# The token tile of step s+2 turned at a step's head through the projection bank, and copied before the SiLU

## What is computed

```python
x = L0_attn_x                                   # 8 x 512 x 256, float32
xn = _layernorm(x, axis=-1)
x = x + mamba(xn) + experts(xn)

# mamba: in-projection to 512 (a half is the gate), causal convolution of 4 taps,
# SiLU, projections to B, C (16 each) and dt; then for 16 states of each channel
#   h = h * exp(dt * A) + dt * B * x;   y = sum(h * C) + x * D
# over 512 tokens; y * silu(gate); out-projection; layernorm(out + xn)

# experts: 8 experts, 2 per token, hidden width 1024
logits = silu(xt @ rw1 + rb1) @ rw2 + rb2       # top 2 are kept, softmax over them
h = silu(xt @ we1[e] + be1[e]);  eo = h @ we2[e] + be2[e]
y = xt + sum over the token's 2 experts of weight * eo
```

## Time and profile before

| | us |
|---|---|
| median of 3 timed runs | 930.38 (929.67 to 933.92) |
| the profiled execution's time | 937.38 |
| its span, first to last instruction | 935.0 |
| TensorE busy | 790.0 (84%) |
| VectorE busy | 781.6 (84%) |
| ScalarE busy | 664.7 (71%) |
| GpSimd busy | 601.8 (64%) |

### The profile page before, as it was taken

One profiled execution on the slowest core, in us unless ns is written; L12 is line 12 of the kernel. 1 busy time (PEld: TensorE's weight loads), 2 busy tenths in 40 slices (PEclk: granted clock), 3 DMA queues, 4 the chain that ended last, 5 costly groups with the idle time before them and its releaser, 6 DMA issues.

```text
span 935.0 us, 14382 instructions
## 1 busy us (share of the span) xinstructions
PE 790.0 (84%) x4533; PEld 639.3 (68%) x4533; DVE 781.6 (84%) x774; ACT 664.7 (71%) x1134; POOL 601.8 (64%) x384
## 2 busy tenths in 40 slices
PE   3994859898998899889988998989988998899852
PEld 2662648777776778677866887677767786778741
DVE  6818857997989988997899699969898789969993
ACT  1433677858688778876887779686887788769930
POOL 3571525676478747774777756785687487758861
PEclk9996979998999999989999999999999999999985
DMA  9939446577657876787579775776588667877741
GB/s 298 388 142 343 178 135 222 184 222 226 185 181 220 254 224 204 218 249 217 187 209 260 240 221 176 234 260 197 168 222 281 189 216 205 252 214 235 230 90 22
DMA packets 81927, 201.00 MB, mean 215 GB/s; under 512 B 7936, under 2 KB 41216, under 8 KB 81728
## 3 DMA queue, kind: packets, MB, share of 16 engines
q1 hardware_dynamic: 61424, 171.46, 53.9%
q0 software_dynamic: 19168, 26.59, 15.0%
q10 hardware_dynamic: 1264, 2.05, 0.7%
HBM read 174.38 MB, written 26.61 MB: 215 GB/s over the span
## 4 chain that ended last, share of the span: by engine, by line
PE 32%; DVE 31%; issue 9%; ACT 9%; DMA 8%; SPq 2%; POOL 1%; DVEq 0%; ACTq 0%; POOLq 0%
PE ps_up L1248 14%; DVE ps_drive L954 11%; PE ps_yx L1262 8%; DVE ring L961 8%; DVE ps_drive L947 6%; DMA bc_scratch<-sp 6%; PE ps_fr L1179 4%; ACT L805 3%; DVE xx L928 2%; ACT da L778 2%; PE ps_up L1242 2%; DMA out<-yo,sid 2%; PE ps_fr L1204 1%; SPq L527 1%; DMA xg<-xn_scratch,gid 1%
## 5 line engine op out<-in xcount | busy, mean ns | idle before, releaser
L598 POOL TENSOR_TENSOR y<-y,ring 128x1024 f32<-128x1024 f32 x126 | 326.2, 2589 | 61.6 <-ACT y L769 54.2
L954 DVE TENSOR_TENSOR_SCAN ps_drive<-da,ps_drive 128x1024 f32<-128x1024 f32 x128 | 293.7, 2295 | 57.8 <-ACT da L778 54.2
L1248 PEld LDWEIGHTS ps_up<-xgt,w1s 128*128 128x128 f32 x2272 | 290.9, 200 | 18.8 <-issue 9.6
L1248 PE MATMUL ps_up<-xgt,w1s 128*128 128x128 f32 x2272 | 290.3, 283 | 0.0
L1262 PE MATMUL ps_yx<-w,ht 128*128 x1136 | 270.6, 381 | 0.0
L1262 PEld LDWEIGHTS ps_yx<-w,ht 128*128 128x128 f32 x1136 | 206.4, 191 | 28.7 <-issue 5.0
L587 POOL DMA_INDIRECT out<-yo,sid x71 | 115.6, 1628 | 145.1 <-ACT yo L820 98.2
L805 ACT ACT_TABLE_LOAD x143 | 183.5, 1283 | 2.5
L778 ACT ACTIVATE da<-gd,col 128x511 f32<-128x511 f32 x256 | 168.3, 710 | 0.0
L947 DVE TENSOR_TENSOR ps_drive<-ps_u,rep 128x1024 f32<-128x1024 f32 x128 | 157.4, 1229 | 9.5 <-DVE ring L961 0.5
L961 DVE TENSOR_TENSOR ring<-ps_drive,rep 128x1024 f32<-128x1024 f32 x128 | 156.5, 1223 | 3.9
(11 more groups left out here) (172 smaller groups left out, 720.4 us busy)
## 6 DMA issues: line engine op xcount, KB each, us to landing
w1s<-in_we SPq DMA_DIRECT2D x71, 1024.0 KB, 7.3
rep<-bc_scratch SPq DMA_DIRECT2D x128, 512.0 KB, 4.7
w<-in_we SPq DMA_DIRECT2D x8, 1024.0 KB, 12.0
w<-in_x SPq DMA_DIRECT2D x8, 512.0 KB, 11.1
xn_scratch<-da SPq DMA_DIRECT2D x8, 512.0 KB, 7.0
out<-w POOLq DMA_DIRECT2D x8, 512.0 KB, 6.4
xnt_scratch<-xx SPq DMA_DIRECT2D x8, 512.0 KB, 5.9
xx<-xnt_scratch SPq DMA_DIRECT2D x8, 512.0 KB, 3.5
```

The lines of the kernel that those rows point to most:

```text
L598: pool.tensor_tensor(y[:, :, :], y[:, :, :], ring[:, g % RING, :, :], ALU.add).then_inc(s_sum, 1)
L954: dve.tensor_tensor_scan(states, da[:, g % DECAYS, :, :].rearrange("p k l -> p (k l)"), states, 0.0, ALU.mult, ALU.add).then_inc(s_scanned, 1)
L1248: mm = pe.matmul(bank[:, c * P:(c + 1) * P], w1s[:, q, k, at:at + P], xgt[:, k, :], start=False, stop=(c == 3 and k == KD - 1))
```

## The change

- For tiles whose step of turning is 2 to 8 of a block (`at_head`), `turn_x(s+2)` moves from the middle of `down(s)` to the head of step s, ahead of `up(s+1, 0)`, and writes to the left half of `ps_fr` instead of up0. It waits until all uses of `ps_fr` before it are read and until the copy of tile s+1 is done. Every later use of `ps_fr` waits for the copy of the last tile turned there (`bank_free`).
- For the same tiles `copy_x(s+2)` moves on ScalarE from behind the Exp table to between the SiLU table and `hidden(s+1, 0)`.
- `xgt` gets two buffers, so the copy waits for `up(s)` instead of `up(s+1)`; `xg` gets three, and the gather is issued one tile sooner (s+4 in step s).
- In steps 0 and 1 turning and copying stay where they were.

```diff
+        def at_head(j):
+            return j >= 2 and (j - 2) % STEPS >= 2
...
                 def copy_x(j):
                     act.wait_ge(s_x_turned, j + 1)
-                    if positive(j):
-                        act.wait_ge(s_up_ready, j * 2)
+                    if j >= 2:
+                        act.wait_ge(s_up_ready, j * 2 - 2)
...
                         table_of(ACT.Silu)
+                        if s + 2 < MT and at_head(s + 2):
+                            copy_x(s + 2)
                         for h in range(2):
...
-                    if s + 2 < MT:
+                    if s + 2 < MT and not at_head(s + 2):
                         copy_x(s + 2)
...
+                def bank_free(f):
                     if positive(f):
                         pe.wait_ge(s_fr_read, f)
+                    if last_turned[0] > 0:
+                        pe.wait_ge(s_x_copied, last_turned[0])
+                    used[0] = f + 1
+
+                def project(at, rows_out, f, src):
+                    bank_free(f)
...
                 def turn_x(j):
...
+                    if at_head(j):
+                        pe.wait_ge(s_fr_read, used[0])
+                        pe.wait_ge(s_x_copied, j)
+                        last_turned[0] = j + 1
+                    elif j > 0:
                         pe.wait_ge(s_hidden, j * 2 - 1)
...
+                    if s + 2 < MT and at_head(s + 2):
+                        turn_x(s + 2)
                     if s + 1 < MT:
                         up(b, i + 1, e_next, 0)
```

More of the change, by code:

```diff
@@ L34 @@
 HBUF = 2
+XGS = 3
 assert STEPS % WBUF == 0
@@ L106, in build @@
         xtok = sb("xtok", [P, TB, D])
-        xg = sb("xg", [P, 2, D])
-        xgt = sb("xgt", [P, KD, P])
+        xg = sb("xg", [P, XGS, D])
+        xgt = sb("xgt", [P, 2, KD, P])
         rep = sb("rep", [P, REPS, 2, L])
@@ L471, in build @@
         s_ln_scaled = sem("s_ln_scaled")
-        s_gathered = [sem(f"s_gathered{q}") for q in range(2)]
+        s_gathered = [sem(f"s_gathered{q}") for q in range(XGS)]
         s_x_turned = sem("s_x_turned")
@@ L498, in build, with turned @@
         front = {use: n for n, use in enumerate(uses)}
+        def at_head(j):
+            return j >= 2 and (j - 2) % STEPS >= 2
+        def turned(j):
+            return psum["fr"][:, 0:D] if at_head(j) else tr_x
         def positive(n):
@@ L575, in gather @@
                     pool.wait_ge(s_tables, 2)
[L576 to L579, removed]
+                    if j >= XGS:
+                        pool.wait_ge(s_x_turned, j - XGS + 1)
+                    pool.indirect_dma_start(xg[:, j % XGS, :], None, xn_d[:, :],
+                                            bass.IndirectOffsetOnAxis(ap=gid[:, j:j + 1], axis=0)).then_inc(s_gathered[j % XGS], 16)
                 def scatter(s, b, i):
@@ L638, in step @@
                     s = b * STEPS + i
-                    if s + 3 < MT:
-                        gather(s + 3)
+                    if s + 4 < MT:
+                        gather(s + 4)
                     if i < IN and not (last and i == IN - 1):
@@ L672, in _ @@
                 pool.wait_ge(s_tables, 2)
-                for j in range(3):
+                for j in range(4):
                     gather(j)
@@ L682, in _ @@
                                    accum_op=ALU.add).then_inc(s_out_rows, 16)
-                for q in range(2):
-                    pool.wait_ge(s_gathered[q], 16 * ((MT + 1 - q) // 2))
+                for q in range(XGS):
+                    pool.wait_ge(s_gathered[q], 16 * ((MT + XGS - 1 - q) // XGS))
                 pool.wait_ge(s_scattered, 16 * MT)
@@ L782, in copy_x @@
                     act.wait_ge(s_x_turned, j + 1)
-                    if positive(j):
-                        act.wait_ge(s_up_ready, j * 2)
-                    act.activation(xgt[:, :, :], tr_x.rearrange("p (k c) -> p k c", k=KD), ACT.Copy).then_inc(s_x_copied, 1)
+                    if j >= 2:
+                        act.wait_ge(s_up_ready, j * 2 - 2)
+                    act.activation(xgt[:, j % 2, :, :], turned(j).rearrange("p (k c) -> p k c", k=KD), ACT.Copy).then_inc(s_x_copied, 1)
                 def weights_in(n):
@@ L1196, in proj_out @@
                     pe.wait_ge(s_y_gated, b + 1)
-                    pe.wait_ge(s_fr_read, front["out", b, half])
+                    bank_free(front["out", b, half])
                     for c in range(2):
@@ L1210, in last_out @@
                     if j == 0:
-                        pe.wait_ge(s_fr_read, front["out", B - 2, 1] + 3)
+                        bank_free(front["out", B - 2, 1] + 3)
                     if j in (1, 2):
@@ L1247, in up @@
                         for k in range(KD):
-                            mm = pe.matmul(bank[:, c * P:(c + 1) * P], w1s[:, q, k, at:at + P], xgt[:, k, :],
+                            mm = pe.matmul(bank[:, c * P:(c + 1) * P], w1s[:, q, k, at:at + P], xgt[:, j % 2, k, :],
                                            start=False, stop=(c == 3 and k == KD - 1))
```

8 lines of the change are left out of this document (4 added, 4 removed).

## The result

The changed kernel takes **982.0 us** (median; 979.4 to 989.7, 6 runs) where the kernel before, timed beside it, takes 930.57 us (929.67 to 933.92, 6 runs): a ratio of 1.0545, 95% interval 1.0514 to 1.0575. The change costs some 51 us. Predicted were 969 us with a range of 944 to 992.

What follows compares the result with a forecast made beforehand. It took a PE-ACT-DVE chain through step 2's tap, the store and the tail as the bound. Six blocks at +6.7 us (5.1 loop, 1.6 clock) and block 0 at -1.5 made +38.7 on 930.38: 969 us, range 944 to 992.

Steps and rivals of the forecast that it cites:

- The loop of copies: Steps 2 to 6: ACT's copy and PE's projection take turns; copy to copy 12.3, 13.9, 11.5 and 14.8 us.
- The scatter in step 4: ACT's way from step 4 to 5: a 1.3 us wait for the scatter kept, 11.5 us in all.
- The clock: Behind step 5's new pause of some 6 us, PE's clock falls: 1.6 us a block, from 0 to 3.
- Step 3's pause: PE's pause of 2.7 us in step 3: 0 for the clock, 1.6 us at the upper end.
- Block 0: Copies 4.9 us sooner, store still sets `dt_in(1)`: 2.1 late, tail 2.0 and clock 1.6 less, -1.5 us.
- Block 4: Forecast like all of blocks 1 to 6: 6.7 us longer, near 105.8 us from scan to scan.
- My upper end: 8.3 us plus two us for `gated` and the output projection behind later scatters: 10.3 x 6 = 62 us.
- The tail's gain: Second `dt_in` to next scan: turn waits only for dt's read, copy leaves the chain; 2.0 us a block.
- The way of 12.0 us: Step 7's way to the SiLU in the tail: 12.0 us at full speed, 13.6 before at the lower clock.
- rival D: ACT copies before PE reaches the projection; tail gives 2.0 and clock 1.6 in 7 blocks: 905 us, 9%.
- The block sum: Whole kernel: 6 x 6.7 us for blocks 1 to 6, -1.5 for block 0, 0 for block 7: +38.7.
- The first chain: Step 2's projection waits for ACT's copy, delaying SiLU, L706 and tap by 2.1 us; later steps build up.

Runs made afterwards that it cites:

- e6: The changed kernel with 24 more matmuls, whose result is overwritten, in TensorE's pause of step 5: 985.59 us, ratio 1.0606.
- e8: e4 without the load of the Exp table in step 7 and of the SiLU table in step 8: 921.51 us, ratio 0.9866.
- e4: The changed kernel with ScalarE's copy at the head of its step, ahead of the decays and the SiLU table: 921.26 us, ratio 0.9889.
- e1: The changed kernel with no tile turned at the head; the added buffers and the early gather stay: 931.84 us, ratio 0.999.
- e2: The changed kernel with the tile of step 2 turned and copied where it was before: 967.28 us, ratio 1.0391.
- e3: The changed kernel with the head turn only for the tiles of steps 4, 7 and 8: 928.7 us, ratio 0.9963.
- e11: The changed kernel with the sum of a finished block into the output moved from step 4 to step 6: 1047.06 us, ratio 1.1243.
- e7: The changed kernel with the head turn only for the tiles of steps 2 and 3: 989.26 us, ratio 1.0605.

## Why the prediction was right, and where not

**The loop of copies.** ScalarE's copies of block 3, on the time axis of the earlier trace rows (14.72 us off):

| | predicted | measured |
|---|---|---|
| copy of step 2 | 459.2 | 459.25 |
| step 3 | 471.5 | 471.59 |
| step 4 | 485.3 | 485.53 |
| step 5 | 496.8 | 495.62 |
| step 6 | 511.6, with 1.6 of clock 513.2 | 513.14 |
| second `dt_in` | 516.5, with the clock 518.1 | 518.14 |
| tail | 18.6 | 18.53 |
| blocks 1, 2, 3, 5, 6 | 105.8 | 105.50 to 105.78 |

The prices from the rows of before carry the steps from copy to copy. That the whole block came out to within 0.3 us is in part luck, since two terms were off against each other, by 1.4 and 1.1 us. **The scatter in step 4**: I kept 1.3 us of wait in ScalarE's way from step 4 to 5; it took 10.09 instead of 11.5, so the wait wasn't there. **The clock**: from the copy of step 5 to that of step 6 it took 17.52, 2.7 over the 14.8, where I had 1.6. The rows at the lower level are the `bc` projection, 3.59 instead of 1.96, and the `up` behind it, 2.81 instead of 1.95.

**Step 3's pause.** I took 0 for the clock there, and 1.6 us at the upper end. In the changed kernel its projection was slow in blocks 0 and 4 (3.4 and 3.5 us) and not in the five others, so 0 was the likelier value and no certain one; e6 shows the fall in five blocks of seven. Where it came, it cost 1.7 us from step 3's projection to step 5's.

**Block 0 failed**: -1.5 predicted, +0.69 measured. The step was that the store still sets `dt_in(1)` there. Its head is 84.18 against 80.37 us, and the store isn't waited for: block 0's own loop is longer than the store, and the slow projection of step 3 adds to it. In e6, where step 3 stays fast in block 0, the head is 82.93 us and the store isn't waited for either. **Block 4 failed** too: 109.80, where the sum gives 106.2. PE waits for the gated `y` behind the first scan of every block, 1.73 us in block 3 and 2.22 in block 4, and only in block 4 the clock is low behind it. The granted clock is the third number from the end, in block 4 and at the same place of block 3:

```profile
554.00:558.00 4.00, 4.00 (x14) 2.92 (x14) 2.70 (x3) 3.18 (x5) 2.51 (x3) 0.57 0.58 145
```

```profile
448.20:452.20 4.00, 4.00 (x29) 3.56 (x28) 3.90 (x4) 3.23 (x5) 2.91 (x3) 1.00 0.59 166
```

Step 2's projection comes 31.05 us after the first scan there instead of 28.87, and step 3's fall adds 1.7. My upper end had two us for `gated` and the later scatters, but as a wait; a clock term at that place I didn't have. Block 7 came a us shorter.

**The tail's gain** was 2.06 us, as predicted, though its reason was half right. I let PE's way end it and ScalarE's own an estimated us sooner. In the rows ScalarE works from 532.86 to the scan with hardly a gap, and its last SiLUs run as one pair without a wait; e8 shows that in e4's tail PE's way ends within 0.1 us of ScalarE's. The way of 12.0 us "at full speed" was also too short. Block 1 of before, in which the clock stayed up there, has a tail of 20.34, and block 3, in which it fell, 20.59; e1's blocks have the same two numbers. So in that tail the slow clock cost 0.25 us and not 1.6. That is why e4 is not at the 905 of rival D, which had 2.0 and 1.6 a block: its blocks 0 to 6 take 96.5 us on average and e1's 98.7, 15.4 us in all, of which block 7 and the start, 2.9 and 1.0 us longer, take back some.

**The total.** The block sum was +38.7; the blocks give 44.4, and of the difference 3.6 are block 4's and 2.2 block 0's. The sum was laid on the median of before, 930.4, while its prices came from an execution at 937.4. The changed kernel's profiled execution lies 1.3 us under its own median. The two are the other part of the 13 us by which the point was low: such a difference should have been laid on the profiled execution, or the uncertainty named. e1 has a profiled execution near the median, 931.06 us; its blocks 0 to 6 take 691.0 us, and the changed kernel's are 50.0 longer, not 44.4.

**The mechanism and what the rows of it hid.** The first chain (copy, projection, SiLU) was named right: e1, e2 and e3 bear it out within their numbers, and e4 in its sign. What I missed is the second: I had the later scatters as two us on `gated` in the upper end, and not that a transfer would take twice as long at its new time, with a scatter, a weighing and the next block's dt behind it. In the changed kernel both chains are about equally long: in block 3 the weighing of tile 6 waits 0.34 us for the scatter (537.21), and e11's block 1 gained nothing without that chain. Where something shortens the head, the second chain can be seen taking over: the weighing waits 1.94 us in e6's block 5, and 1.40 and 2.73 us in e2's blocks 3 and 5, whose tails are 0.9 and 3.8 us longer than the changed kernel's. How much of e6's lack of gain is due to it and how much to the clock in steps 3 and 0 stays open: I didn't run the fill with a short landing.

## What to carry to other kernels

When a copy moves ahead of a matmul in a shared bank, put it ahead of the work of the copying engine that nobody awaits: here step 2's copy at 25.6 us into the block instead of 28.4, and its fellows, were worth 61 us in all. Where a wait is predicted to go away or to move, list every transfer that a later instruction must see landed, and ask what will go out beside it at its new time. And read a block that the disturbance has not reached yet: one such block told more here than the time of the whole kernel.

## What the runs showed of the hardware

- The sum into the output (512 KB, accumulating) lands in 6.7 us (median) in the kernel before, where a 1 MB load follows it 3.4 to 5.5 us later, and in 11.0 and 12.7 us in the changed kernel and e7, where the load follows within 2.4 us. Why is not shown.
- After a pause of TensorE of 2.58 us, at the same place of the same kernel, the lower granted clock came in some blocks and not in others: in 2 of 7 blocks of the changed kernel and in 5 of 7 of e6. After a pause of 5.4 to 6.5 us it came in 6 of 6 blocks of the changed kernel (3.59 us for a projection that takes 1.88 in e6).
- With step 5's pause filled, step 3's slow projection came in more blocks (5 of 7 instead of 2). Whether the fill brought that on is not shown.
